# Second expert layer: routing and scattering moved into the causal attention

## The reference

```python
t = t + _L3_attn_ref(_ln_t(t), w_qkv, w_out)   # causal attention within an image, 8 heads of 16
t = t + _L3_ffn_ref(_ln_t(t), W_router, W1, b1, W2, b2)

# _L3_ffn_ref, x_flat = normalised tokens, 4096 rows of 128
logits = x_flat @ W_router                     # 8 experts
topk_p, topk_i = top_k(softmax(logits), 2)
topk_p = topk_p / topk_p.sum(-1)
for e in range(8):
    h = relu(x_flat @ W1[e] + b1[e])           # 128 -> 512
    y = h @ W2[e] + b2[e]                      # 512 -> 128
    out = out + combine[:, e] * y
```

## Time and profile before

| | |
|---|---|
| median of 3 runs | 1587.54 us (1586.53 to 1589.31) |
| profiled execution, own time | 1590.38 us |
| its span | 1588.5 us |
| PE, DVE, ACT, POOL busy | 1155.0, 830.2, 665.1, 595.4 us |
| instructions | 31046 |

### The profile page before, as it was taken

The page is one execution under the profiler, slowest core; times in us unless marked ns, Lnnn a source line. Parts: engine busy times, 40 slices in busy tenths (PEclk is TensorE's granted clock), DMA queues, the critical chain, the costliest instruction groups (busy, mean ns, idle before and its releaser), DMA issues. The chain is left out here.

```text
span 1588.5 us, 31046 instructions
## 1 busy us (share of the span) xinstructions
PE 1155.0 (73%) x9416; PEld 919.0 (58%) x9416; DVE 830.2 (52%) x2572; ACT 665.1 (42%) x1430; POOL 595.4 (37%) x832
## 2 busy tenths in 40 slices
PE   4539786888879664238999996488999750079992
PEld 3439452545557661026999996256666450069991
DVE  5654796634677545015555553556555350056774
ACT  2323573644555432015666663124444330045651
POOL 5500341155655324730244443111222217746660
PEclk9759998998999766559999998579999755589995
DMA  2139201000000071100111111200000021112225
GB/s 71 39 75 184 46 27 35 16 13 9 9 4 2 2 303 52 52 28 14 36 47 48 48 46 41 74 27 2 1 2 2 5 116 53 52 49 62 63 61 165
DMA packets 91154, 78.76 MB, mean 50 GB/s; under 512 B 21808, under 2 KB 84016, under 8 KB 89776
## 3 DMA queue, kind: packets, MB, share of 16 engines
q1 hardware_dynamic: 81072, 56.98, 13.9%
q0 software_dynamic: 9984, 20.53, 3.9%
HBM read 44.29 MB, written 33.18 MB: 49 GB/s over the span
## 5 line engine op out<-in xcount | busy, mean ns | idle before, releaser
L1787 POOL DMA_INDIRECT ys_scratch<-m_yout,m_xin x152 | 162.2, 1067 | 245.5 <-DVE m_yout L1889 193.5
L1821 PE MATMUL m_eps_up<-m_ext,m_w_up 128*128 128x128 f32 x1856 | 240.2, 280 | 0.9 <-DVE m_w_up L1868 0.8
L1821 PEld LDWEIGHTS m_eps_up<-m_ext,m_w_up 128*128 128x128 f32 x1856 | 224.3, 195 | 3.7 <-issue 1.3
L1831 PE MATMUL m_eps_y<-m_w_down,m_ht 128*128 128x128 f32 x1216 | 161.2, 276 | 0.6 <-DVE m_ht L1881 0.5
L1629 POOL DMA_INDIRECT xs_scratch<-m_xn,m_slot x128 | 123.8, 967 | 94.5 <-issue 38.4
L1842 ACT ACTIVATE m_w_up<-m_up 128x512 f32 x152 | 95.7, 630 | 141.0 <-PEq L1600 91.5
L1831 PEld LDWEIGHTS m_eps_y<-m_w_down,m_ht 128*128 128x128 f32 x1216 | 148.6, 193 | 1.0 <-DVE m_ht L1881 0.7
L2085 POOL TENSOR_SCALAR_AFFINE_SELECT c_e<-c_e 128x256 f32<-128x256 f32 x128 | 49.4, 410 | 202.7 <-ACT c_e L2118 202.7
L1811 PE MATMUL m_eps_x<-ident,m_xin 128*128 128x128 f32 x152 | 44.0, 289 | 103.8 <-DMA m_xin<-xs_scratch 102.8
L1293 POOL TENSOR_TENSOR a_z<-a_y,a_peak 128x16 f32<-128x16 f32 (+31 forms) x64 | 67.7, 1058 | 105.3 <-DVE a_peak L1204 93.7
L2176 DVE TENSOR_REDUCE c_peak<-c_ps_s 128x2 f32<-128x256 f32 (+1 forms) x128 | 65.4, 554 | 72.7 <-PE c_ps_s L2298 72.7
(11 more groups left out here) (326 smaller groups left out, 2554.2 us busy)
## 6 DMA issues: line engine op xcount, KB each, us to landing
xs_scratch<-empty SPq DMA_DIRECT2D x20, 516.0 KB, 11.4
m_xin<-xs_scratch SPq DMA_DIRECT2D x152, 64.5 KB, 1.8
m_y<-ys_scratch SPq DMA_DIRECT2D x22, 256.0 KB, 5.2
m_up<-in_m_gate SPq DMA_DIRECT2D x2, 2048.0 KB, 14.2
m_up<-in_m_up SPq DMA_DIRECT2D x2, 2048.0 KB, 18.6
m_down<-in_m_down SPq DMA_DIRECT2D x2, 2048.0 KB, 23.3
a_q_in<-q_scratch SPq DMA_DIRECT2D x80, 32.0 KB, 1.7
c_rows<-ys_scratch SPq DMA_DIRECT2D x10, 256.0 KB
```

The costliest lines, as they stand in the source:

```text
L1787: pool.indirect_dma_start(ys_dram, bass.IndirectOffsetOnAxis(xin[:, u, C:C + 1].bitcast(U32), 0), yout[:, u, :], None).then_inc(stored[u], 16)
L1821: last = pe.matmul(ps[u % 2][:, k * P:(k + 1) * P], w[:, u % 2, k * P:(k + 1) * P], xt[:, u % 2, :], start=True, stop=True)
L1831: last = pe.matmul(ps_y[u % 2][:, 0:C], ht[:, u % 2, k, :], w_down[:, u % 4, k, :], start=(k == 0), stop=(k == KC - 1))
```

## The change

`route` and `dispatch` are no longer called for the second expert layer. Their work is done by image inside `causal_attention`, behind the image's own attention. Each expert gets a fixed region of 4096 + 128 rows in `xs_scratch`, so a slot is the region's start plus a running rank, and no total is needed. Images are ranked in lots: seven lots of two images, then two of one. The variance's inverse root is taken on POOL with `pow`. After the loop the counts give, for each of the 72 tiles, its expert and its first row (`row_of`), which SP reads into a register ahead of each load; and SP copies 128 dummy rows behind each region's last row, DRAM to DRAM. The fill in the convolution keeps the first layer's ten transfers and has two for the second layer. PE's order within a step is changed, so that each of the four `score` units of a step stands next to a `rescore` unit in the other half of the rows.

```diff
 # POOL, inside causal_attention: constants ahead of the loop
+            for k in range(TOPK):
+                pool.iota(xn3[k][:, :, C].bitcast(I32), ...)
+            pool.memset(...) x4, pool.iota(...) x3, pool.affine_select(triangle), pool.tensor_copy(...) x3
-            for n in range(UN * B):           # the cuts, in order
+            def invert(b):
+                pool.tensor_scalar(var3[:], mv3[:, b % 2, :, 1], 1e-5, None, ALU.add)
+                pool.tensor_tensor(scale3[:, 2 * b:2 * b + 2], var3[:], power[:], ALU.pow)
+            def copy_rows(b):
+                pool.tensor_copy(xn3[1][:, 2 * b:2 * b + 2, 0:C], xn3[0][:, 2 * b:2 * b + 2, 0:C])
+            def send(b, first, end):          # four indirect DMAs an image
+                if first == 0: wait slot_ready of the lot, copied3 of the image
+            for i in range(-2, B + 10):
+                cut_off(i - 2, 3); cut_off(i - 1, 0); send(i - 9, 0, 1)
+                cut_off(i - 1, 1); invert(i - 4);     send(i - 9, 1, 3)
+                cut_off(i - 1, 2); send(i - 9, 3, 4); copy_rows(i - 5)
 # ACT
-            drain(i-2) exp(i-1,0) exp(i-1,1) q_copy k_copy(i+1) norm(i+2) exp(i-1,2) ot_copy(i-2) exp(i-1,3)
+            exp(i-2,3) exp(i-1,0) norm3(i-5) drain(i-2) exp(i-1,1) norm(i+2) xt3_copy(i-5) exp(i-1,2)
+            q_copy k_copy(i+1) ot_copy(i-2)
 # DVE (lot: image i-6 ends a lot; ranking: image i-7 ends a lot)
+            dve.wait_ge(const3, CONSTS3 + 1)  # ahead of the loop
-            top(i,0) lower(i-1) add(i-3) top(i,1) x_out(i+1) o_norm(i-2) top(i,2) count(i-3) v_copy(i+1) top(i,3)
+            top(i,0) lg_copy(i-6) lower(i-1) add(i-3) top(i,1) x_out(i+1) spread3(i-4) choose(lot,0)
+            top(i,2) take_rank(ranking) o_norm(i-2) choose(lot,1) top(i,3) v_copy(i+1) join(lot)
+            slots(ranking) shift_of(i-4) count(i-3)
+            # choose(lot,0): 5 steps; choose(lot,1): 6; join: 3; take_rank: 1; slots: 4, on [128, 4, 8]
+            # after the loop: gap, tables (17 steps), weights (3 steps)
 # PE
-            score(i,0) turn_peak(i-1) weigh(i-2,1) score(i,1) turn_x(i+1) rescore(i-1,0) turn_back(i-2)
-            score(i,2) rescore(i-1,1) project(i+1) score(i,3) rescore(i-1,2) weigh(i-1,0) turn_o(i-2)
-            rescore(i-1,3) project_o(i-2)
+            logits_of(i-6) score(i,0) rescore(i-2,3) project_o(i-3) turn_peak(i-1) score(i,1) rescore(i-1,0)
+            turn_x(i+1) weigh(i-2,1) rank_of(lot of i-7) score(i,2) rescore(i-1,1) turn_back(i-2) turn3(i-5)
+            score(i,3) rescore(i-1,2) project(i+1) weigh(i-1,0) turn_o(i-2)
+            # turn3: 2 transposes; logits_of: 2 matmuls to 8 columns; rank_of: 5 matmuls of at most 32 columns
 # SP, inside causal_attention, behind the fetches of the first layer's late results
+            sp.dma_start(w3[:], router); load_experts(sp, nxt, *loads); sp.wait_ge(pads_ready, 1)
+            for e_no in range(E):
+                at = sp.value_load(pad_at[0:1, e_no:e_no + 1], ...)
+                sp.dma_start(xs_dram[bass.ds(at, P), :], xs_dram[spare:spare + P, :])
 # experts
-                sp.dma_start(xin[:, u, :], xs_dram[bass.ds(j * P, P), :])
+                row = j * P if m.swiglu else sp.value_load(m.row_of[0:1, bass.ds(j, 1)], ...)
+                sp.dma_start(xin[:, u, :], xs_dram[bass.ds(row, P), :])
```

More of the change, by code:

```diff
@@ new lines, in causal_attention @@
+        same = s.sb("n_same", [P, 4, E])
+        low = s.sb("n_low", [P, 4, E])
+        idx = s.sb("n_idx", [P, TOPK, 4])
+        pick = s.sb("n_pick", [P, 2, 4, TOPK, E])
+        both = s.sb("n_both", [P, 2, 4, E])
+        own = s.sb("n_own", [P, E])
+        so_far = s.sb("n_so_far", [P, 2, E])
+        rank = s.sb("n_rank", [P, 4, E])
+        part = s.sb("n_part", [P, 4, TOPK, E])
+        slot_f = s.sb("n_slot_f", [P, 4, TOPK])
+        order_i = s.sb("n_order_i", [P, E], I32)
+        order = s.sb("n_order", [P, E])
@@ L2037, in causal_attention @@
+        sent = [s.sem(f"n_sent{i}") for i in range(4)]
+        CONSTS3 = 10
         early_norm = TokenNorm(s, keep, "norm3", 0, EARLY)
@@ L2248, in _ @@
                     late_norm.collect(dve)
+            dve.tensor_tensor(gap[:], nxt.peak[:, 1, :], nxt.peak[:, 0, :], ALU.subtract).then_inc(gap_ready, 1)
+            tables()
+            weights()
         @block.tensor
@@ new lines, in logits_of @@
+            def logits_of(b, units):
+                pe.wait_ge(xt3_ready, b + 1)
+                pe.wait_ge(peaked, 2 * units)
+                unread()
+                for h in range(2):
+                    last = pe.matmul(ps_s[:, 0, SPAN + h * E:SPAN + (h + 1) * E], xt3[:, b % 2, h * P:(h + 1) * P], w3[:],
+                                     start=True, stop=True)
+                last.then_inc(logits3, 1)
+                written["logits"] += 1
+                if units == UN * B:
+                    asked.update(written)
@@ L2284, in score, with total_of @@
+            def total_of():
+                pe.wait_ge(both_ready, 2 * len(LOTS))
+                unread()
+                pe.matmul(ps_s[:, 0, SPAN:SPAN + E], ones[:], so_far[:, len(LOTS) % 2, :], start=True, stop=True).then_inc(totalled, 1)
             def score(b, u):
@@ new lines, in hybrid @@
+        m2 = Moe(lasting, "m2", 16, True)
+        with ExitStack() as layer:
+            own = Space(nc, layer, keep.spent)
+            m2.load_into(own)
+            with ExitStack() as rows:
+                space = Space(nc, rows, keep.spent)
+                xn = [space.sb(f"m2_xn{k}", [P, NT, ROW]) for k in range(TOPK)]
+                loads = [a["m2_gate"], a["m2_up"]], a["m2_down"]
+                route(nc, own, m2, a["m2_router"], lambda sp: load_experts(sp, m2, *loads), xn, keep)
+                dispatch(nc, own, m2, xs_drams[0], xn, (a["m2_shared_up"], a["m2_shared_down"]), keep)
+            experts(nc, own, m2, xs_drams[0], ys_dram, keep)
```

459 lines of the change are left out of this document (359 added, 100 removed).

## The result

The changed kernel takes 1525.28 us (median of 5 runs, 1522.4 to 1532.76), the kernel before 1587.54 beside it: a ratio of 0.9604 [0.9572, 0.9636], 62 us less. The forecast was 1511, its whole range 1497 to 1532, its own narrower one 1503 to 1521. So the direction and most of the size came as forecast, and the time lies 14 us above the number and 4 above the narrower range.

The account below looks back on a forecast made before the run. POOL alone bounds the gap between attention and experts, PE the attention. Experts start 78.2 us earlier, register load +2: -76.2 us from 1590.38 gives 1514.2, 1511 at the median; range 1497 to 1532.

Parts of the forecast that it names:

- POOL alone between attention and experts, gone but for eight images' scatters: Between attention and experts: after the last cut only 32 scatters of 1.265 us and small instructions remain, 43.2 us.
- No wait for slots, tables in the slack: After the last cut: image 15's routing is ready before POOL asks for it, slack 16 us; tables take about 5.3 us.
- SP's eight copies in the same slack: After the last cut: SP's eight copies end within the 16 us slack of image 15's routing.
- Pairing -14.1 us: Attention steps: score beside rescore saves 0.79 us a pair; two more pairs a step gain 11.1 and 3 us.
- PE's additions and waits, 13.3 + 2 + 2.5 us in the loop: Attention loop: transposes, logits and ranks add 13.3 us, queue waits 2 us, DVE late in odd steps 2.5 us.
- Behind the last projection +3 us: Attention steps 16 and 17: PE's additions put about 3 us more ahead of the last cut.
- The attention's sum of +7.9 us: Attention, last cut later: 1.2 - 14.1 + 13.3 + 3 + 2 + 2.5 = +7.9 us.
- Register load in the experts +2 us: Second expert layer: SP's register load, 0 to 0.4 us in the buffer ring, costs +2 us, bounds 0 and +9.
- rivals D and E: Scatters beside DVE: slow at 1.2 us each, 1519 us, 5%; or POOL held in every one, slower than before, 4%.
- Rival A: Attention: pairs cost nothing, both save fully (-23 us), no step waits; about 1498 us, chance 12%.
- B: Attention: DVE becomes the bound, 21 us instead of 2.5; 1530 us, chance 13%.
- F: After the last cut: image 15's routing is later than POOL's 38 us by some us; 1517 us, chance 3%.

Follow-up runs that it names:

- e2: Changed kernel with the eight copies of the spare rows shared, four issued by ScalarE and four by SyncE; 1526.8 us, ratio 0.9615.
- e4: Kernel before with only the new paired order of the attention on TensorE, ScalarE and VectorE, routing and scatters untouched; 1576.26 us, ratio 0.9924.
- e1: Changed kernel with SyncE reading the tile's first row into a register ahead of its wait for the buffer; 1516.43 us, ratio 0.956.
- e5: Changed kernel with the register load of the tile's first row done twice, both behind the wait for the buffer; 1535.28 us, ratio 0.9676.
- e6: Changed kernel with the eight registers of the spare-row copies loaded first and the copies issued after them, all on SP; 1520.08 us (two runs only).
- e7: Changed kernel with row read ahead of the wait, spare-row copies on two engines, fetched rows added before the copy of the values; 1496.45 us, ratio 0.9435.
- e12: Kernel with the three edits together, plus the four fetched rows of each early step spread over VectorE's step; 1488.49 us, ratio 0.938.
- e3: Changed kernel with the fetched rows of the first expert layer added before the copy of the values in VectorE's order; 1505.48 us, ratio 0.9481.

## Why the prediction was nearly right, step by step

- **POOL alone between attention and experts, gone but for eight images' scatters: right.** 43.2 us forecast, 45.3 measured. The 1.265 us of a scatter held, but for one scatter of 1.44 us and a few tenths after each inversion. The small instructions were mis-sized: an inversion puts 1.0 us between two scatters (`pow` alone takes 0.72) and a row copy 0.28, together 4.2 us where 2.7 was taken; the bound of 1 us each held.
- **No wait for slots, tables in the slack: right.** The tables' last step ends at 1308.95, 10.7 us ahead of the last scatter's end. **SP's eight copies in the same slack: wrong.** They are issued until 1327, 7.5 us behind it. By the gaps with and without e2's edit this costs about 1.5 us; by its duration 0.6 us more is the first tile's register load, an estimate that no run separates. That leaves 1.0 us of the 12.1; the same handover took 10.9 to 12.0 us in four other traces.
- **Pairing -14.1 us: too large, by two errors of opposite sign and one step left out.** The pair of unit 1 was thought to lose 0.6 of its 0.79 us to the lowering, and lost 0.2. But I added savings of PE as if PE stayed the bound; at 12.45 us it waits 0.54 us a step. And the first five steps got 4.7 us longer, not shorter: TensorE waits 21.8 us for peaks there, 15.3 before. No sentence of the prediction spoke of these steps' own limits, the 4.3 us of fetched rows in VectorE's queue among them. The rows explain the level (16 us in either order) but not the pairs' loss, which stays at 4.6 us with the rows moved; its cause is open. The 5.8 us won at the end were not in the sum either. Measured: -8.7 us.
- **PE's additions and waits, 13.3 + 2 + 2.5 us in the loop: too large.** Between e4 and the changed kernel the ten periods of images 5 to 15 grew by 8.7 us, 0.43 without a ranking, 1.66 with one. Logits (0.37), turns (0.38) and ranks (1.14) are as sized, but some of them fill the waits that the pairs opened. That DVE would be late in the odd steps isn't seen as more than 0.5 us (the mask of unit 3 waits 0.48).
- **Behind the last projection +3 us: too small.** Between e4 and the changed kernel it is +9.0 us: 3.5 for the clock's fall and 5.5 for the work and its waits. The errors in the additions partly cancel: 17.7 us measured with the last line, about 21 forecast.
- **The attention's sum of +7.9 us: met, by luck.** In the traces of e1, e2, e5 and e6, which leave it as it is, the attention takes 258.6 us in the mean (250.3 before), and the prologue adds 0.5: +8.8 us. But the pairs were taken 5.4 us too high and the additions nearly 4 us too high, and only their difference came out. Most of the 14 us between 1511 and 1525 lies behind the attention.
- **Register load in the experts +2 us: the largest miss, 7.4 us.** The mechanism (a ring of eight, load behind store) was named and its far bound of +9 us nearly met. What failed are the load's price and "it binds only part of the time": at 0.4 us even a ring that always binds gives 3.6 us, the load takes 0.6 us on SyncE, and by the means of the traces it costs about 8. The slack was also read too large: 152/72 = 2.11 us a tile counts the end of the stage in, while the turns of the kernel before come 143.7/71 = 2.02 us apart.
- **Scatters beside DVE (rivals D and E): they fell.** In the attention a scatter takes 0.96 to 1.10 us, with VectorE busy 65% of the steady part. The estimate that made the change lose took the factor of the example in the Trainium skill ("SBUF — State Buffer", the "DVE blocks DMA" trap) for every scatter; the page ties the block to VectorE copies in a two-port mode. The measurement decides: no indirect DMA of the changed kernel's trace takes over 1.44 us. Rival A had part of the truth (unit 1), B and F none.

## What to carry to other kernels

When a step is moved in one engine's order, follow its result to the consumer and read what stands behind that consumer in its queue: here moving 4.3 us of unrelated work a step ahead of a copy was worth 16 us, paired or not, more than the 12 that the pairs won. About half of that was TensorE's clock, which rose with the shorter waits; so price a wait with what it does to the clock of the work behind it. A register load belongs ahead of the wait of its DMA, not behind it: in a ring of buffers it costs more than its own duration. And a bound that is relieved gives back only up to the next one, so savings of an engine are summed only as long as it has no wait in the period.

## What the runs showed of the hardware that was not expected

- A register load with its check takes SyncE about 0.6 us ahead of a DMA (0.27 for TENSOR_LOAD, 0.15 for the arithmetic behind it; the experts' first turns come 1.1 us apart, 0.59 in the kernel before). During the last scatters the same instructions, and moves of 0.03 us, took up to 0.7 or 0.8 us each, on ScalarE's queue too, and were back at 0.03 to 0.27 about 3 us behind the last scatter. Whether the scatters cause it was not tested. Scatters as such are not enough: beside those of the experts' results, one for each tile, all 72 loads of e6 took 0.26 to 0.28 us.
- GpSimd's `pow` on 128x2 elements takes 0.72 us, an addition of the same size 0.22 to 0.25.
- With the same instructions in the last two attention steps, TensorE's clock stayed at 2.4 GHz in two traces (e7, e12) and fell to 1.2 in six (the changed kernel, e1, e2, e3, e5, e6), with PE busy 3.14 (e7) and 3.22 (the changed kernel) of 4 us in the windows at that point.
- In the attention's first five steps the granted clock went from 0.75 to 0.87 of full speed when VectorE's order alone was changed, and PE's busy time for the same matmuls from 72.5 to 63.6 us.
